# Causal attention stage of a two-layer encoder kernel: the instruction order of a block rewritten on TensorE, VectorE and ScalarE

## The reference

```python
x = x + xattn0(layernorm(x), ctx, ctx, mask)          # stage A
x = x + moe_encoder(layernorm(x), ...)                # stage B: 2 of 4 experts for each sequence
x = x + causal_attention(layernorm(x), ctx, ctx, Wq, ..., Wo, bo)   # stage C, 16 heads of 16
x = x + shared_and_routed_ffn(layernorm(x), ...)      # shared part beside stage C, routed part at the end

# stage C, for one sequence
scores = q @ k.T / sqrt(16) + causal
out    = softmax(scores) @ v @ Wo.T + bo
# shared part of the last step
sh = layernorm(silu(x @ sw1.T + sb1) * (x @ sw2.T + sb2)) * g + b
shared_out = sh @ sw3.T + sb3
```

## Time and profile before

| | |
|---|---|
| median of 3 runs | 836.39 us (835.06 to 837.0) |
| the profiled execution | 835.16 us, its span 833.4 us |
| TensorE busy | 723.0 us, 87% |
| VectorE busy | 650.1 us, 78% |
| ScalarE busy | 337.4 us, 40% |
| GpSimd busy | 379.1 us, 45% |
| mean granted TensorE clock | 0.923 |

### The profile page before, as it was taken

The page is one execution under the profiler, slowest core; times in us unless marked ns, Lnnn a source line. Parts: engine busy times, 40 slices in busy tenths (PEclk is TensorE's granted clock), DMA queues, the critical chain, the costliest instruction groups (busy, mean ns, idle before and its releaser), DMA issues.

```text
span 833.4 us, 29134 instructions
## 1 busy us (share of the span) xinstructions
PE 723.0 (87%) x10978; PEld 571.7 (69%) x10978; DVE 650.1 (78%) x1858; ACT 337.4 (40%) x710; POOL 379.1 (45%) x647
## 2 busy tenths in 40 slices
PE   4788469999999999999999999998889888734895
PEld 3567447888888888888888888876556656412673
DVE  4786556787878788887877888789999999845965
ACT  4656224444343444434343444434445545412200
POOL 2788712435353454535444453543345345254132
PEclk9766589999999999999999999999999999955797
DMA  7776300000000000000000000002221222122000
GB/s 272 244 238 226 140 2 2 4 2 4 2 3 3 2 4 3 3 3 3 3 4 3 3 4 9 9 22 73 91 89 60 78 90 80 32 86 75 5 1 6
DMA packets 24655, 41.24 MB, mean 49 GB/s; under 512 B 3727, under 2 KB 16665, under 8 KB 24267
## 3 DMA queue, kind: packets, MB, share of 16 engines
q1 hardware_dynamic: 23096, 37.39, 13.6%
q0 software_dynamic: 704, 1.71, 0.8%
q10 hardware_dynamic: 726, 0.30, 0.1%
HBM read 30.86 MB, written 8.91 MB: 48 GB/s over the span
## 4 chain that ended last, share of the span: by engine, by line
PE 69%; DVE 17%; POOL 5%; issue 5%; ACT 4%; DMA 1%; POOLq 0%; ACTq 0%; DVEq 0%; SPq 0%
PE ps L480 7%; PE ps L474 7%; PE ps L482 6%; PE ps L481 6%; PE ps L684 6%; PE ps L666 5%; DVE mx L1403 5%; PE ps L616 4%; PE ps L722 3%; PE ps L724 3%; PE ps L723 3%; PE ps L618 3%; PE ps L617 3%; PE ps L608 2%; POOL w_lo L1826 2%
## 5 line engine op out<-in xcount | busy, mean ns | idle before, releaser
L1040 ACT ACTIVATE pT<-ps 128x1024 f32<-128x1024 f32 x96 | 93.1, 1022 | 124.5 <-PE ps L666 124.5
L1799 POOL TENSOR_TENSOR rs<-mv,cst 128x1 f32<-128x1 f32 x132 | 31.2, 236 | 178.6 <-DVE mv L1174 140.9
L1403 DVE TENSOR_REDUCE mx<-ps 128x16 f32<-128x2048 f32 x48 | 109.4, 2280 | 1.0 <-PE ps L639 1.0
L1887 POOL TENSOR_TENSOR y<-y,vec 128x256 f32<-128x256 f32 x32 | 23.2, 726 | 170.7 <-DVE y L1177 170.7
L722 PE MATMUL ps<-xh,w_hi 128*128 128x128 bf16 x512 | 99.4, 219 | 0.0
L723 PE MATMUL ps<-xl,w_hi 128*128 128x128 bf16 x512 | 99.3, 219 | 0.0
L724 PE MATMUL ps<-xh,w_lo 128*128 128x128 bf16 x512 | 99.3, 219 | 0.0
L1801 POOL TENSOR_TENSOR rs<-rs,cst 128x1 f32<-128x1 f32 x132 | 73.2, 554 | 10.3
L480 PE MATMUL ps<-w_hi,hh 128*128 x256 | 69.8, 273 | 0.0
L481 PE MATMUL ps<-w_hi,hl 128*128 x256 | 69.8, 273 | 0.0
L482 PE MATMUL ps<-w_lo,hh 128*128 x256 | 69.8, 273 | 0.0
(11 more groups left out here) (366 smaller groups left out, 2495.1 us busy)
## 6 DMA issues: line engine op xcount, KB each, us to landing
stage<-in_w SPq DMA_DIRECT2D x32, 384.0 KB, 3.7
vec<-in_vec SPq DMA_DIRECT2D x4, 896.0 KB, 5.8
vec<-in_tw SPq DMA_DIRECT2D x12, 256.0 KB, 2.8
ctxc<-in_ctx SPq DMA_DIRECT2D x19, 128.0 KB, 2.2
comb<-x SPq DMA_DIRECT2D x16, 128.0 KB, 1.7
comb<-t SPq DMA_DIRECT2D x16, 128.0 KB, 1.8
shared<-x1b SPq DMA_DIRECT2D x16, 128.0 KB, 1.7
out<-x SPq DMA_DIRECT2D x16, 128.0 KB, 1.8
```

The source lines that it names most:

```text
L1040: A(pT[:, 8 * a:8 * a + 8, :].rearrange("p h q -> p (h q)"), ps[:, 2 * a:2 * a + 2, :].rearrange("p g k -> p (g k)"), ACT.Exp, scale=SCALE ...
L1403: nc.vector.tensor_reduce(mx[:, :], att.rearrange("p g s k -> p (g s) k"), AX.X, ALU.max, negate=True).then_inc(m_max, 1)
```

## The change

The operations and their number stay the same (PE 8605 and DVE 1863 rows in the program's order, in both). Their order within `block_c` changes on three engines:

- **TensorE:** `scores(m)` stands right behind `projection_v`, ahead of the second half of `values`, and waits for pT_b. `prep`, `shift_transpose` and `scores_T` come ahead of `sh_first`, `sh_z` and `out_proj`. `scores_T` writes the masks of banks 1, 2 and 3 before it waits for the shift, whose transposed form lies in bank 0, and for the second pieces of q and k.
- **VectorE:** `maxima` and `shift_split` follow `qk_low` directly. `sh_zlow` now serves b - 4 and stands ahead of `bias_v`. `sh_silu` moves from ahead of `sh_y` to behind `o_low`; `x3` stands behind `sh_silu` and `sh_gate`.
- **ScalarE:** `sh_zhi` serves b - 4 and `sh_e` serves b - 2, both in the first half of the block; `prep` and `shift` come ahead of `oo`.

```diff
--- before.py
+++ after.py
@@ -648,12 +648,15 @@
             def scores_T(u, causal):
 
 
-                pe.wait_ge(qk_split, u + 1)
-                pe.wait_ge(mT_sb, u + 1)
                 if causal:
-                    for g in range(4):
+                    for g in (1, 2, 3, 0):
+                        if g == 0:
+                            pe.wait_ge(mT_sb, u + 1)
                         mm(ps[:, g, :], identb[:, :], causb[:, 1:2, :].broadcast_to([128, 4, 128]),
                            start=True, stop=False)
+                else:
+                    pe.wait_ge(mT_sb, u + 1)
+                pe.wait_ge(qk_split, u + 1)
                 for c in range(KC):
                     for s in range(2):
                         terms = ((khm, qh), (khm, ql), (klm, qh), (None, None))
@@ -810,11 +813,13 @@
                 if served(b):
                     values(n, slot, 0)
                 if more:
-                    if not isinstance(b, int) or b >= 4:
+                    if b >= 4:
                         pe.wait_ge(s_zsplit, b + (A1 - 4))
                     elif b < 2:
                         pe.wait_ge(hl_b, m - 2)
                     projection_v(None)
+                    pe.wait_ge(pT_b, n + 1)
+                    scores(m, True)
                 if served(b):
                     values(n, slot, 1)
                 if ex is not None:
@@ -828,26 +833,24 @@
                     sh_transposes(b - 1)
                 if served(b):
                     o_rows(n)
+                if served(b + 2):
+                    pe.wait_ge(qk_split, m + 1)
+                    prep(b + (B + 2), True)
                 if more:
-                    scores(m, True)
+                    shift_transpose(m)
+                if served(b):
+                    o_transposes(n)
+                if more:
+                    scores_T(m, True)
                 if served(b - 1):
                     if ex is not None:
                         pe.wait_ge(sw_ready, 2)
                         pe.wait_ge(res2, UNITS)
                     sh_first(b - 1)
-                if served(b + 2):
-                    pe.wait_ge(qk_split, m + 1)
-                    prep(b + (B + 2), True)
-                if served(b):
-                    o_transposes(n)
-                if more:
-                    shift_transpose(m)
                 if served(b - 3):
                     sh_z(b - 3)
                 if served(b):
                     out_proj(n, None)
-                if more:
-                    scores_T(m, True)
 
             pe.wait_ge(g_words, 1)
             pe.wait_ge(w_lo_ready, PAIRS * 3)
@@ -1102,24 +1105,24 @@
                 n, m = b + UNITS, b + (UNITS + 1)
                 if served(b):
                     exps(n)
+                if served(b - 4):
+                    sh_zhi(b - 4)
                 if served(b + 1):
                     qk_hi(m)
+                if served(b - 2):
+                    sh_e(b - 2)
                 if served(b):
                     o_evict(n)
                 if served(b - 1):
                     sh_y(b - 1)
                 if weights is not None:
                     tw(*weights)
+                if served(b + 2):
+                    prep(b + (B + 2), 2 * KC)
+                if served(b + 1):
+                    shift(m)
                 if served(b):
                     oo(n)
-                if served(b + 1):
-                    shift(m)
-                if served(b - 3):
-                    sh_zhi(b - 3)
-                if served(b + 2):
-                    prep(b + (B + 2), 2 * KC)
-                if served(b - 1):
-                    sh_e(b - 1)
 
             for n in range(-1, UNITS + 1):
                 block(n, prep_of(n + 2))
@@ -1582,51 +1585,48 @@
             def block_c(b, slot):
 
                 n, m = b + UNITS, b + (UNITS + 1)
-                rest = n if isinstance(n, int) else 2 * UNITS
                 if served(b - 1):
                     stats_c(b - 1)
                 if served(b + 3):
                     y_stats_of(at(b + 3), b + (B + 3))
-                if served(b - 2):
-                    sh_silu(b - 2)
                 if served(b - 1):
                     sh_y(b - 1)
-                if rest - 4 < UNITS:
-                    add_expert(rest - 4, at((rest - 4) // 2))
-                if rest - 3 < UNITS:
-                    norm2(rest - 3, 1 - slot)
+                if n - 4 < UNITS:
+                    add_expert(n - 4, at((n - 4) // 2))
+                if n - 3 < UNITS:
+                    norm2(n - 3, 1 - slot)
                 if served(b - 3):
                     sh_gnorm(b - 3)
+                if served(b - 4):
+                    sh_zlow(b - 4)
                 if served(b + 1):
                     bias_v(m, 1 - slot, vc[:, VC_V:VC_V + D])
                     qk_low(m)
-                if served(b - 4):
-                    sh_sum(b - 4)
-                if served(b):
-                    o_norm(n)
-                if served(b - 1):
-                    if rest - 2 < UNITS:
-                        sum2(rest - 2, slot)
-                    sh_low(b - 1)
-                if served(b - 2):
-                    sh_gate(b - 2)
-                if served(b + 1):
                     maxima(m)
                     shift_split(m)
                 if served(b):
+                    o_norm(n)
+                if n - 2 < UNITS:
+                    sum2(n - 2, slot)
+                if served(b + 2):
+                    y_low(b + (B + 2), 2 * KC)
+                if served(b - 4):
+                    sh_sum(b - 4)
+                if served(b - 1):
+                    sh_low(b - 1)
+                if served(b):
                     o_low(n)
-                if rest - 2 < UNITS:
-                    stats2(rest - 2, slot)
+                if served(b - 2):
+                    sh_silu(b - 2)
+                    sh_gate(b - 2)
+                if served(b):
+                    x3(n, b, slot)
+                if n - 2 < UNITS:
+                    stats2(n - 2, slot)
                 if served(b - 2):
                     sh_gstats(b - 2)
-                if served(b - 3):
-                    sh_zlow(b - 3)
-                if served(b):
-                    x3(n, b, slot)
                 if served(b - 1):
                     sh_bias(b - 1)
-                if served(b + 2):
-                    y_low(b + (B + 2), 2 * KC)
                 if served(b + 3):
                     y_of(at(b + 3), b + (B + 3), UNITS)
 
```

## The result

The changed kernel takes 870.73 us (median of 4 runs, 868.76 to 871.12), the kernel before 835.72 us beside it (834.76 to 837.0): a ratio of 1.0413 (95% interval 1.0391 to 1.0436), 4.1% slower. The forecast was 874 us, with a range of 858 to 885.

What follows compares the result with a forecast made beforehand. VectorE was taken to bound the kernel, with 11.56 us of work in a 12.13 us block. Waits 27.4 plus clock 10.8 = 38.2 us on 835.16 gave 873.4, and 874 us with the runs' median; range 858 to 885.

Steps and rivals of the forecast that it cites:

- A block can't fall below 11.56 us: Stage C: VectorE's work is 11.56 of a 12.13 us block, so the largest gain is 0.57 us per block.
- The four waits: New VectorE waits per block: sh_y 0.42, sh_gnorm 0.46 (GpSimd's roots), bias_v 0.98 (projection_v), x3 0.79 us (out_proj).
- The block: Stage C block: 11.56 us of VectorE work plus the four waits gives 14.21 us, 2.08 more than before.
- The first blocks and the end: Block 1 -2.7, blocks 2 and 3 +0.8 together; end: x3(14) 3.6, block 15's roots 1.0, behind token gathers 2.2 us.
- Blocks 4 to 14: Steady blocks at full clock: blocks 4 to 13 cost 10 x 2.08 = 20.8 us, block 14 costs 1.7.
- The clock: TensorE's 2.40 us stall ahead of projection_v halves its clock: 1.2 us in 9 of 11 blocks, 10.8 us; bounds 0 and 21.
- The shared activation beside GpSimd: sh_silu's product and sh_gate beside GpSimd's work: up to 0.7 us longer, costed at nothing; at most 4 us without cover.
- A clock that holds (864): Rival: the waits come as laid out and TensorE's clock stays full, 864 us; chance 0.28.
- The dearest case (889): Rival: clock falls in every block at full price and GpSimd blocks VectorE's products, 889 us; chance 0.07.
- Faster through a shorter chain: Rival: the long chain breaks and VectorE's new waits stay below 0.57 us per block, 828 us at best; chance 0.06.
- Half of the waits merging: Rival: an early wait in a block lets later results ripen, 11 x 1.0 + 5, some 852 us; chance 0.08.
- No change (836): Rival: the long chain is shortened and the waits refill it exactly, 836 us; chance 0.03.

Runs made afterwards that it cites:

- the first three edits: Single edits to the changed kernel: sh_zlow ahead of sh_y (855.25 us), sh_gnorm behind the split (859.65 us), out_proj directly behind scores_T (856.84 us).
- sh_zlow early: Changed kernel with sh_zlow(b-4) moved on VectorE from behind sh_gnorm to behind y_stats_of, ahead of sh_y: 855.25 us, ratio 1.0209.
- sh_gnorm late: Changed kernel with sh_gnorm moved on VectorE from ahead of sh_zlow to behind the maxima and the split: 859.65 us, ratio 1.0271.
- twelve new orders: The changed kernel (870.73 us) and the eleven follow-up kernels, which measured from 832.19 to 874.11 us.
- out_proj first: Changed kernel with out_proj moved on TensorE from behind sh_z to directly behind scores_T, ahead of sh_first: 856.84 us, ratio 1.0253.
- the maxima ahead: Kernel before with only scores moved right behind projection_v, and maxima and split right behind qk_low: 862.04 us, ratio 1.0316.
- the best order: Changed kernel with three edits, bias_v and qk_low as cover ahead of sh_y, projection_v ahead of values, and GpSimd's x_bias and weight piece moved earlier: 832.19 us, ratio 0.9955.
- as sh_silu showed: Changed kernel with sh_silu put back ahead of sh_y on VectorE, and sh_e for b-1 back to the end of ScalarE's block: 874.11 us, ratio 1.0460.
- the GpSimd move on the kernel before: Kernel before with x_bias and the weight piece moved ahead of GpSimd's shared affine, and ScalarE's half ahead of o_evict: 835.60 us, ratio 0.9997.
- the order with cover: Changed kernel with three edits, bias_v and qk_low ahead of sh_y, projection_v ahead of values: 841.91 us; with x_bias and weight piece moved on GpSimd, 832.19 us.

## Why the prediction was right, step by step

- **A block can't fall below 11.56 us; all else can only add waits.** Right, and shown from the other side: the order in which every wait has cover and no product is held up takes 11.56 us. That the two agree to 0.01 us is partly chance, since sh_silu takes 1.57 us there (649.40 to 650.97) and 1.43 in the kernel before.
- **The four waits.** Forecast 0.42, 0.46, 0.98 and 0.79 us, measured 0.37, 0.44, 0.92 and 0.47. Each has its own source: the first three edits took away the one that each was aimed at and left the others, but for two side effects (sh_zlow early halved sh_y's, and with sh_gnorm late x3's was filled by a longer product). TensorE's stall ahead of projection_v was forecast at 2.40 us and is 2.33. The term that is off is the last, x3. Its chain was right (4.88 forecast, 4.77 measured); what was short is VectorE's work ahead of it, 4.09 forecast and 653.11 - 648.81 = 4.30 measured. That is sh_silu, whose step is 1.65 us (651.17 to 652.82) and not 1.43. Half of it is the first instruction, most of that held up beside GpSimd (0.31 us and not 0.19), the other half the product, whose step is 0.32 us and not 0.21: the kernel has sh_gate wait for it, and sh_gate now follows directly.
- **The block.** Forecast 14.21, measured 14.09. It is closer than its parts: the four waits sum to 2.20 us and not 2.65, and the rest of the block is 11.89 us and not 11.56, of which sh_silu is 0.22; for the other 0.11 I have no row.
- **The first blocks and the end.** Block 1: -2.2, forecast -2.7. Blocks 2 and 3: +3.15 together, forecast +0.8; x3(1) waits 2.23 us, since no sh_silu stands ahead of it yet, and the clock fell in the second of them, where x3(2) waits 2.24. Behind the last maxima: 6.85, forecast 3.6 + 1.0 + 2.2 = 6.8. The forecast gives no rows for these three nor for the -2.7 and the +0.8, and only the sum of the three is compared here, not each.
- **Blocks 4 to 14.** At full clock they are 19.9 us longer, forecast 20.8 + 1.7 = 22.5. The block is 0.12 us shorter than forecast, and the kernel before already loses 0.63 us in each of its last two, where the gate product takes 1.00 and 0.99 us beside the weight piece; the forecast took 12.13 us for them all.
- **The clock.** Forecast nine falls in eleven blocks at 1.2 us. Measured seven falls, in six blocks, none of them before the stage's end in the kernel before. Five of these blocks are 0.35, 0.54, 1.13, 1.35 and (with two falls) 2.71 us longer than 14.09: 6.1 us, for 10.8 forecast. This term was mis-sized, and its reason is only half right: the 2.33 us stall comes in every block and the clock falls behind some of them. With the stall cut to 0.74 us it still fell three times in steady blocks. The dear bound, 11 x 1.9 = 21, doesn't follow from the text's own most of 1.72 us, which gives 19; the price of one fall stayed below both.
- **The shared activation beside GpSimd, costed at nothing.** Right for this kernel and by luck of the order: there the products are clear of GpSimd's (both lines lie between 0.291 and 0.293 us in all 16 calls), and only the first instruction of sh_silu is touched. In five of the experiments that product or the gate product is 0.3 to 0.9 us longer. The Trainium skill (SBUF — State Buffer, section "Who interferes with whom") has the later of two such instructions blocked for the whole of the other; the traces agree, with an end 0.13 to 0.16 us behind the other's. The prediction says that the median of the earlier trace rows doesn't agree, and that reading is wrong: in the block of the earlier trace rows GpSimd's sum ends at 657.37 and the gate product, 0.36 us long from 657.15, at 657.51, so the median is the wait for the rest of the sum.
- **Rivals.** A clock that holds (864): out, it fell. The dearest case (889): out, falls were fewer. Faster through a shorter chain: out, the four waits sum to 2.20 us where VectorE lost 0.57 before. Half of the waits merging: out in the steady block, 2.20 of 2.65 us came. No change (836): out.

The terms sum to 27.4 + 10.8 = 38.2 us; measured are 35.4, of which 1.64 lie ahead of the stage and belong to no term. Of the other 33.8 us, 6.1 are the clock and 27.7 the rest. That the rest comes so close to 27.4 is luck: blocks 1 to 3 (one fall among them) are 2.8 us dearer than forecast and blocks 4 to 14 are 2.6 us cheaper. The miss that stays is the clock's price, 4.7 us too high.

## What stays open

What exactly lets the clock fall. Eight of the twelve new orders have a fall in the blocks that begin the stage. Behind block 4 it fell four times with a stall of 2.33 us in each block, three times behind stalls of 1.09, 1.10 and 1.66 us (sh_zlow early), and not at all with 1.71 (sh_gnorm late), 1.77 (out_proj first) or 1.49 us (the kernel before). With the maxima ahead and 2.21 us it fell twice. So the length of the longest stall doesn't order these, and no run varied one alone.

Also open is where the best order loses what its blocks gain: its 14 blocks are 8.4 us shorter than those of before, and the whole is 3.4 us faster in the median, 1.5 us in the two profiled executions (831.9 and 833.4). Of the 6.9 us between, 2.5 lie ahead of the stage, which the order doesn't touch, and 4.3 in the stretch behind its last maxima, 118.3 us long (831.9 - 713.58); I didn't take that apart.

## What to carry to other kernels

When one engine is at 95% of a block, lay its instructions end to end in the new order, and ask of each what it waits for and what stood there as cover before: four such waits gave the block within 1%, part of which was two errors that cancel. Waits with sources of their own can be removed singly, but their cover can be spent only once, as sh_silu showed. And look beside the engine too: an edit that moves nothing on GpSimd can still shift it in time, so compare durations of the same instruction, not only waits.

## What the hardware showed unexpectedly

A VectorE product of two SBUF tensors (128x128, 0.29 us alone) that starts while GpSimd runs such a product (0.72 to 1.21 us) ends 0.13 to 0.16 us behind it, up to 1.20 us long. Beside the small product of a root (128x1, 0.55 us) it isn't held up: with the GpSimd move on the kernel before, the gate product starts inside one at 597.47 and takes 0.28 us. In the other direction less is lost: w_lo takes 1.20 to 1.22 us where such a VectorE product runs at its start, and 1.15 to 1.17 elsewhere. Of instructions that read one SBUF tensor, sh_silu's first (0.19 us ahead of sh_y, 0.22 in its new place) became up to 0.50 in a steady block and up to 1.05 at the stage's end, and a normalization (0.35) 0.76 to 1.20, each ending 0.07 to 0.10 us behind GpSimd's; the reciprocal kept its 0.95 us wherever it met one. With an operand in PSUM, bias_v, qk_low and the maxima kept their length: the maxima take 2.28 to 2.29 us in all 48 calls of every trace, beside the weight piece or not. The line of the gate product in the order with cover, without and then with the move on GpSimd; minimum, median and maximum in ns:

```profile
L1564 DVE TENSOR_TENSOR h<-h x16: 291/1130/1136, 577.9 to 762.2; 128x128 f32<-128x128 f32 x16
```

```profile
L1564 DVE TENSOR_TENSOR h<-h x16: 291/291/293, 579.1 to 752.0; 128x128 f32<-128x128 f32 x16
```
